# Neighbour sums of a graph network: a running sum at fixed addresses on VectorE, copied to its node tile by ScalarE

## The reference, cut to what matters

```python
agg = jax.ops.segment_sum(x[src], dst, num_segments=n)
h = x + agg                                   # the two convolutions of layer 0
h = relu(_batchnorm(h @ W1 + b1, gamma, beta))
```

## Time and profile before

| what | value |
|---|---|
| median of 3 runs | 7780.57 us (7720.62 to 7806.80) |
| the profiled execution, its own time | 7720.02 us |
| its span | 7718.3 us |
| mean granted TensorE clock | 0.757 of full speed |
| PE, PEld busy | 65%, 41% of the span |
| DVE, ACT, POOL busy | 46%, 19%, 44% |

### The profile page before, as it was taken

One profiled execution on the slowest core, in us unless ns is written; L12 is line 12 of the kernel. 1 busy time (PEld: TensorE's weight loads), 2 busy tenths in 40 slices (PEclk: granted clock), 3 DMA queues, 4 the chain that ended last, 5 costly groups with the idle time before them and its releaser, 6 DMA issues. The chain is left out here.

```text
span 7718.3 us, 88077 instructions
## 1 busy us (share of the span) xinstructions
PE 5026.5 (65%) x17714; PEld 3164.4 (41%) x17715; DVE 3543.2 (46%) x8494; ACT 1478.3 (19%) x3917; POOL 3405.8 (44%) x3530
## 2 busy tenths in 40 slices
PE   2265565666658577767775399489998647665445
PEld 0011232323334323335564278467775423232244
DVE  7387343433344566655556211355555532233512
ACT  0001000200032366631111122123333212000011
POOL 1710777376600166656662355435551030477422
PEclk6587665766679689977767599789999778666767
DMA  3100333233300000012222267323331043333235
GB/s 147 51 5 28 91 94 91 61 93 90 89 16 0 21 2 1 1 47 80 79 79 41 71 201 225 104 86 98 94 98 37 0 132 99 104 92 92 57 120 174
DMA packets 402784, 596.29 MB, mean 77 GB/s; under 512 B 130985, under 2 KB 305641, under 8 KB 401577
## 3 DMA queue, kind: packets, MB, share of 16 engines
q0 software_dynamic: 147584, 361.63, 16.9%
q1 hardware_dynamic: 255018, 232.69, 10.1%
HBM read 472.89 MB, written 121.17 MB: 77 GB/s over the span
## 5 line engine op out<-in xcount | busy, mean ns | idle before, releaser
L643 PE MATMUL ps<-wide 128*128 128x256 f32 x2640 | 1187.4, 573 | 786.7 <-issue 488.2
L631 POOL DMA_INDIRECT wide<-table,src x880 | 897.7, 1020 | 797.4 <-ACTq L94 435.1
L643 PEld LDWEIGHTS ps<-wide 128*128 128x128 f32 x2640 | 580.1, 261 | 1394.4 <-issue 829.5
L670 DVE TENSOR_TENSOR sums<-sums,ps 128x256 f32 x1320 | 556.0, 421 | 1212.5 <-PE ps L643 472.7
L631 POOL DMA_INDIRECT wide<-table_rel,rel x440 | 450.8, 1025 | 396.7 <-ACTq L94 218.1
L1568 POOL DMA_INDIRECT wide<-table_gat,work x440 | 471.7, 1072 | 307.9 <-ACT work L1544 163.0
L2191 POOL DMA_INDIRECT work<-table,work x440 | 438.9, 998 | 312.0 <-PE ps L2228 167.7
L1452 POOL DMA_INDIRECT work<-table_max,work x440 | 435.1, 989 | 257.2 <-issue 137.2
L1471 PE MATMUL ps<-wide,work 128*128 128x512 f32 x880 | 491.9, 643 | 0.0
L1599 PE MATMUL ps<-wide,work 128*128 128x260 f32 x880 | 353.3, 557 | 87.5 <-DVE sums L1670 72.2
L1435 ACT ACTIVATE wide<-ident,work 128x128 f32<-128x128 f32 x1320 | 398.0, 387 | 5.4 <-DMA work<-table_max,work 4.4
(11 more groups left out here) (431 smaller groups left out, 9401.7 us busy)
## 6 DMA issues: line engine op xcount, KB each, us to landing
wide<-in_L_ffn_W SPq DMA_DIRECT2D x64, 1024.0 KB
wide<-in_L_ffn_expert_w SPq DMA_DIRECT2D x90, 256.0 KB
table_rel<-wide SPq DMA_DIRECT2D x20, 1024.0 KB
work<-rows_in SPq DMA_DIRECT2D x62, 256.0 KB
rows_out<-work SPq DMA_DIRECT2D x62, 256.0 KB
work<-rec SPq DMA_DIRECT2D x110, 136.0 KB
wide<-table,src POOLq DMA_INDIRECT x880
rec<-work POOLq DMA_DIRECT2D x6, 2176.0 KB
```

Source lines behind the costliest of these rows:

```text
L631: nc.gpsimd.indirect_dma_start(rows[:, w % RT, :], None, table, bass.IndirectOffsetOnAxis(ap=index[:, w:w + 1], axis=0)).then_inc(gathered ...
L643: nc.tensor.matmul(m.PS[:, w % (2 * Q), 0:D], S[:, w % RT, :], rows[:, w % RT, :], start=True, stop=True).then_inc(summed, 1)
L670: v.tensor_tensor(at, at, m.PS[:, s, 0:D], ALU.add).then_inc(added, 1)
```

## The change

DVE no longer adds into the node tile. It keeps a running sum in a ring of 8 places at fixed addresses in `m.WS`: place w % 8 becomes (place of w - 1) x same + PSUM bank, by one `scalar_tensor_tensor`. `same1` is 1 where edge tile w has the node tile of w - 1, and 0 where a new one begins; it is a column of 128 equal values for each w, made in `sort_slots`. ACT copies each running sum to the node tile that a register names, so that the last copy of a node tile holds its sum. ACT now loads the registers. PE waits for `run` (DVE's sum) in place of `added`; DVE waits for its own last sum and, from w = 8 on, until ACT has copied what lay in the ring's place (`kept`). ACT waits for the sum and for its own last copy. In `gin` the node features are added in one instruction over all tiles at the end; `store_table` sets `m.AGG` to zero instead of copying. The matmul in `sort_slots` that counts tiles writes 128 rows instead of one.

```diff
@@ sort_slots
-            nc.tensor.matmul(m.PS[0:1, 1, 0:WP], m.ones[0:NT, 0:1], started[0:NT, :], start=True,
+            nc.tensor.matmul(m.PS[:, 1, 0:WP], m.ones[0:NT, :], started[0:NT, :], start=True,
                              stop=True).then_inc(started_up, 1)
...
             c.step(v.tensor_scalar(tn[:], m.PS[0:1, 1, 0:WP], 1.0, None, ALU.subtract))
+            c.step(v.tensor_copy(counted_up, m.PS[:, 1, 0:WP]))
             dve.sem_inc(totalled, 1)
+            v.memset(same[:, 0:1], 0.0)
+            c.step(v.tensor_tensor(same[:, 1:WP], counted_up[:, 1:WP], counted_up[:, 0:WP - 1], ALU.is_equal))
@@ aggregate
-                if w >= 2 * Q:
-                    pe.wait_ge(added, w - 2 * Q + 1)
+                if w >= EIGHT:
+                    pe.wait_ge(run, w - EIGHT + 1)
...
+        @block.scalar
+        def _(act):
+            for k in range(WT // EIGHT):
+                tiles = tile_registers(nc, act, m.tn1[0:1, k * EIGHT:(k + 1) * EIGHT])
+                for s in range(EIGHT):
+                    w = k * EIGHT + s
+                    act.wait_ge(run, w + 1)
+                    if w:
+                        act.wait_ge(kept, w)
+                    nc.scalar.copy(tile_at(m.AGG, tiles[s]), running[:, s, :]).then_inc(kept, 1)
...
-            for k in range(WT // EIGHT):
-                if k + LEAD < WT // EIGHT:
-                    hots(k + LEAD)
-                tiles = tile_registers(nc, dve, m.tn1[0:1, k * EIGHT:(k + 1) * EIGHT])
-                for s in range(EIGHT):
-                    w = k * EIGHT + s
-                    dve.wait_ge(summed, w + 1)
-                    if w:
-                        dve.wait_ge(added, w)
-                    at = tile_at(m.AGG, tiles[s])
-                    v.tensor_tensor(at, at, m.PS[:, s, 0:D], ALU.add).then_inc(added, 1)
+            for w in range(WT):
+                if w % EIGHT == 0 and w // EIGHT + LEAD < WT // EIGHT:
+                    hots(w // EIGHT + LEAD)
+                dve.wait_ge(summed, w + 1)
+                ps = m.PS[:, w % EIGHT, 0:D]
+                if w == 0:
+                    v.tensor_copy(running[:, 0, :], ps).then_inc(run, 1)
+                    continue
+                dve.wait_ge(run, w)
+                if w >= EIGHT:
+                    dve.wait_ge(kept, w - EIGHT + 1)
+                v.scalar_tensor_tensor(running[:, w % EIGHT, :], running[:, (w - 1) % EIGHT, :], m.same1[:, w:w + 1], ps,
+                                       ALU.mult, ALU.add).then_inc(run, 1)
+            if plus is not None:
+                dve.wait_ge(kept, WT)
+                v.tensor_tensor(m.AGG[:, :, 0:D], m.AGG[:, :, 0:D], plus[:], ALU.add)
@@ store_table
-            if sums is None:
-                nc.vector.tensor_copy(m.AGG[:, :, 0:D], src[:])
-            else:
-                nc.vector.memset(m.AGG[:], sums)
+            nc.vector.memset(m.AGG[:], 0.0)
@@ gin
-        aggregate(nc, m, m.table, m.src1)
+        aggregate(nc, m, m.table, m.src1, m.XN)
```

More of the change, by code:

```diff
@@ L197, in setup_memory @@
     m.rel1 = sb("rel1", [P, WP], I32)
+    m.same1, m.same2 = sb("same1", [P, WP]), sb("same2", [P, WP])
     m.tn1 = sb("tn1", [1, WP], I32)
@@ L260, in sort_slots @@
 def sort_slots(nc, m, keys, other, etype, by_source):
-    tn = m.tn2 if by_source else m.tn1
+    tn, same = (m.tn2, m.same2) if by_source else (m.tn1, m.same1)
     TRASH = float(WT * P)
@@ L288, in sort_slots @@
     diagonal, start = take(NT), take(1)
-    started = take(WP)
+    started, counted_up = take(WP), take(WP)
     with Stage(nc) as st:
@@ L612, in tile_registers, with aggregate @@
         skip_runtime_bounds_check_because="a count of node tiles started, less one: tile 0 starts at slot 0, and there are NT")[1]
-def aggregate(nc, m, table, index):
+def aggregate(nc, m, table, index, plus=None):
     with Stage(nc) as st:
-        hot, summed, added = (st.sem(s) for s in ("hot", "summed", "added"))
+        hot, summed, run, kept = (st.sem(s) for s in ("hot", "summed", "run", "kept"))
         R = 8
         RT = R * Q
+        EIGHT = 2 * Q
         gathered = st.sems("gathered", RT)
@@ L623, in aggregate @@
         S = view(m.BB, RT * D, RT, P)
+        running = view(m.WS, 0, EIGHT, D)
         block = st.block()
@@ L637, in _ @@
             for w in range(WT):
-                if w % (2 * Q) == 0:
-                    pe.wait_ge(hot, w // (2 * Q) + 1)
-                if w >= 2 * Q:
-                    pe.wait_ge(added, w - 2 * Q + 1)
+                if w % EIGHT == 0:
+                    pe.wait_ge(hot, w // EIGHT + 1)
+                if w >= EIGHT:
+                    pe.wait_ge(run, w - EIGHT + 1)
                 pe.wait_ge(gathered[w % RT], w // RT * 16 + 16)
-                nc.tensor.matmul(m.PS[:, w % (2 * Q), 0:D], S[:, w % RT, :], rows[:, w % RT, :], start=True, stop=True
+                nc.tensor.matmul(m.PS[:, w % EIGHT, 0:D], S[:, w % RT, :], rows[:, w % RT, :], start=True, stop=True
                                  ).then_inc(summed, 1)
+        @block.scalar
[8 more added lines that the diff above has]
+                    nc.scalar.copy(tile_at(m.AGG, tiles[s]), running[:, s, :]).then_inc(kept, 1)
         @block.vector
@@ L648, in _ @@
             v = nc.vector
-            EIGHT = 2 * Q
             LEAD = 2
@@ L659, in _, with store_table @@
                 hots(k)
-            for k in range(WT // EIGHT):
-                if k + LEAD < WT // EIGHT:
-                    hots(k + LEAD)
-                tiles = tile_registers(nc, dve, m.tn1[0:1, k * EIGHT:(k + 1) * EIGHT])
-                for s in range(EIGHT):
-                    w = k * EIGHT + s
-                    dve.wait_ge(summed, w + 1)
-                    if w:
-                        dve.wait_ge(added, w)
-                    at = tile_at(m.AGG, tiles[s])
-                    v.tensor_tensor(at, at, m.PS[:, s, 0:D], ALU.add).then_inc(added, 1)
-def store_table(nc, m, src, table, sums=None):
+            for w in range(WT):
[14 more added lines that the diff above has]
+                v.tensor_tensor(m.AGG[:, :, 0:D], m.AGG[:, :, 0:D], plus[:], ALU.add)
+def store_table(nc, m, src, table):
     with Stage(nc) as st:
@@ L2120, in edge_update @@
     linear_nodes(nc, m, m.XT, w1[D:2 * D, :], None, D, keep(by_dst))
-    store_table(nc, m, by_dst, m.table, sums=0.0)
+    store_table(nc, m, by_dst, m.table)
     linear_nodes(nc, m, m.XT, w1[0:D, :], a["L2_gnn_b1"], D, keep(by_src))
```

## The result

Over 20 executions the changed kernel has a median of 7812.48 us (7793.89 to 7831.78); the kernel before, run beside it 20 times, has 7783.91 us (7715.00 to 7807.27). The two medians differ by 28.6 us, a factor of 1.0037. The ratio on record, an estimate of its own from the same 40 times, is 1.0059 with a 95% interval of 1.0038 to 1.0081, which is 46 us (30 to 63). The forecast was 7798 us with a range of 7600 to 7880, "no change" within 1% at 0.56: the time lies in the forecast's own range, 14 us above its number. No large effect appeared in either direction.

A forecast was written before the change was run, and what follows sets the result against it. POOL's issue of gathers was taken as the bound, with ring waits what other engines change. Terms 14.3 + 1.8 + 1.4 + 0 = +17.5 us on a median of 7780.6 gave 7798 us, range 7600 to 7880.

The forecast's parts named there:

- The final add: End of a call, in two calls: the add of node features, with nothing to hide behind, 7.1 us each, 14.3 us.
- The add on DVE and the copy on ACT: Per tile in the calls: DVE's sum 0.63 us as before, ACT's copy 0.61 us hidden; last copies add 1.8 us.
- Rival B: ACT's register-addressed copy has long waits of its own; ring waits and tails double: +206 us, 7987 us, chance 0.12.
- sort_slots: Copy from PSUM costs 0.7 us, comparison covered by DVE's wait for PE: 1.4 us in two calls, 2.8 if nothing covered.
- POOL: Gathers in the calls: DVE's new sum with a pointer leaves them at 0.96 us, cost nothing.
- Rival C: The pointer counts as an SBUF operand, so each sum lengthens a gather: +441 us, 8240 us, chance 0.03.
- The long waits: Waits of 5.18 us before DVE's adds in the calls: PE-DVE circle of 8 banks stays, no change, chance 0.56.
- Rivals A and B: A: long waits came from DVE's register-addressed add and vanish, -171 us, 7609 us, chance 0.29. Rival B: its own line.
- The bound: In the calls: POOL's issue, 554 us for 440 gathers; other engines can only change the ring waits, 146 us.
- The sum: Whole kernel: 14.3 + 1.8 + 1.4 + 0 = +17.5 us, giving 7798 us.
- The median: Whole kernel: median of the runs shown taken 60.6 us above the profiled execution of 7720.0 us, so base 7780.6 us.

The follow-up runs named there:

- e7: Changed kernel without running sums, ACT's copies and PE's wait for `run`; gathers, one-hot instructions and matmuls stay: 7669.3 us.
- e8: Changed kernel with the one-hot instruction writing only 8 of 128 columns from its fifth on: 7674.5 us.
- e1: Changed kernel with PE multiplying only 64 of the 256 gathered columns in the neighbour sums: 7692.6 us.
- e9: Changed kernel with PE reading only the upper 16 bits of `S` and `rows`, one weight load and matmul a tile: 7787.94 us, ratio to before 1.0006.
- e4: Changed kernel with two extra bf16 matmuls of 128 columns per tile, ahead of the wait for the gather: 7739.6 us.
- e10: Kernel before with 56 filler bf16 matmuls of 440 columns ahead of the expert stage of `one_expert`: 7722.32 us, ratio 0.9923.

## Why the prediction was right, and where its steps were not

*The final add*: forecast 2 x 7.1 us. The row has 6.82 us and begins 0.02 us behind ACT's last copy and 1.03 us behind DVE's last sum. Taken out, the two gave 17.5 us by the medians and 13.8 by the means. Right.

*The add on DVE and the copy on ACT*: 480 and 405 ns, as forecast from the earlier trace rows. The two rows that priced the pointer, 481 against 425 ns, also differ in reading PSUM or not; L1841 of before, with a pointer and without PSUM, has 485 ns, so the pointer is what costs. The hand-over was cheaper than forecast, 0.57 to 0.58 us a tile instead of 0.63 and 0.61, and as forecast that is worth nothing, since no tile comes so fast but in catching up. ACT's last copy ends 1.0 us after DVE's last sum; forecast was 0.6. Rival B did not come: in all three calls DVE waited 13.1 us for ACT's copies, in 12 waits.

*`sort_slots`*: forecast 0.7 us a call, with the comparison covered by DVE's wait for PE. It was not covered: 1.2 and 1.3 us, 2.5 in all, which is the case of nothing covered (2.8) that the prediction named as the bound.

*POOL*: beside 1317 sums with a pointer its median stays 957 ns, so Rival C did not come. That agrees with the rule of the Trainium skill ("SBUF — State Buffer", Who interferes with whom), if the pointer does not count as an operand in SBUF.

*The long waits, left as they are*: right as a number. The step that failed is the reason given, that PE and DVE go round in a circle of 8 banks; the row that it was read from has PE waiting for "issue", not for DVE. Without DVE's part in it (e7) PE's own four instructions for a tile still take 5.6 us, and a depth of two instead of eight leaves the call as long. The count of finished matmuls is late by itself. Rivals A and B both took the waits to belong to an engine that consumes; no consumer had a part in them, so there was nothing that the change could have removed (A) or doubled (B).

*The bound*: "POOL's issue is the bound, and the waits for the ring are what another engine can add or give back" was half wrong. Issue time that is saved comes back as ring waits (e8, and the change itself: -31 us busy, +36 us waits), and on chips A to C a call of all kernels with matmuls stays at 623 to 633 us (e7's third, 615, is the one below), whatever the matmuls' length and number, DVE and ACT do, and at a clock of 0.50 (e1, e9) as at 0.69 (e4). The mean pace of 1.42 us a tile is set by something else, which shows itself in the late count of finished matmuls. On chip D stages with many indirect transfers were shorter without any edit. What sets the pace stays open. Two rivals were not tested: that it is gathers and PE's reads together, which needs gathers alone and the unaltered kernel profiled on one chip; and that it is the loading of the unrolled code, which needs the same call as a loop.

*The sum*: +17.5 us. In the profiles the calls grew by 17.9 us, but not in the forecast shares: 7.7, 7.7 and 0.6 were forecast and 5.4, 2.5 and 10.0 came, since the tails (14.0, 15.9, 20.2 us from the last gather to the last sum, before 18.2, 22.5, 14.2) vary by more than the terms. So the agreement of 17.9 with 17.5 is luck. The better measures are the timed ones: in the first comparison 29 us between the medians, 25 without the three short executions and 46 by the ratio; on chip B 29 and 25. All are above the forecast, though the interval of the last (17 to 35) reaches it. The term that was too small is the rest beside the final add, 11.7 us on chip B against 3.2; `sort_slots` is 1.1 us of that difference, and where the others lie the scatter does not let me say.

*The median*: I put the profiled execution 60.6 us below the median and took that for the scatter of the runs. It fits the step of 62.7 us in one stage, whose clock before's own windows show (0.86). A reader of the profile alone can't know that this execution is the rare case, but three times of 7721, 7781 and 7807 us were a hint of a step.

## What to carry to other kernels

An idle time with the name of a DMA done long ago, or "issue", means that the cause is not in the list: before building a forecast on a circle of two engines, take one of them away. When saved issue time comes back as waits and the length of the stage stays the same, the named engine is not the bound. Compare profiles stage by stage with the granted clock beside each, because one stage whose clock differs between two executions can be worth more than the change (here 62.7 us against 25 to 29).

## What the runs showed of the hardware that was not expected

- The count of finished matmuls reached DVE some 34 us after the trace had the matmuls (e7). Times between two sums peak at multiples of 0.70 us. The longest are 5.6 us with two weight loads and two matmuls a tile (6.3 us a few times, in before, e8 and e10), 4.2 us with one of each (e9) and 11.2 us with four of each (e4).
- The kernel before took 7149 us on chip D and 7689 to 7784 us on the others; the stretch of `place_edges` took 296 us there and 454 to 476 on the others. All stages that were over 4 us shorter there are ones with 160 or more indirect transfers by POOL.
- The expert stage of `one_expert` took 113 to 114 us at a mean clock of 0.86 and 177 us at 0.50, with identical instructions, and both levels occurred on chip B.
